# A complex linear recurrence on one Trainium2 core: four of ten elementwise instructions of each group on GpSimd, with a second buffer for two tiles

## What is computed

```
x: 8 sequences of 256 tokens, 128 channels
lambda = exp(-nu + i theta),  gamma = sqrt(1 - |lambda|^2 + eps)
Bu[t]  = gamma * (B_re + i B_im) x[t]
h[t]   = lambda * h[t-1] + Bu[t]                    (complex, per channel)
out[t] = Re(C h[t]) + D_skip * x[t]
x      = layernorm(x + out)
```

## Time and profile before

| | |
|---|---|
| median of three runs | 1337.15 us |
| lowest, highest | 1335.71, 1341.49 us |
| span of the profiled execution (first to last instruction) | 1318.2 us |
| TensorE busy, share of the span | 1096.4 us, 83% |
| VectorE busy | 801.6 us, 61% |
| ScalarE busy | 534.2 us, 41% |
| GpSimd busy | 379.6 us, 29% |

### The profile page before, as it was taken

One profiled execution on the slowest core, in us unless ns is written; L12 is line 12 of the kernel. 1 busy time (PEld: TensorE's weight loads), 2 busy tenths in 40 slices (PEclk: granted clock), 3 DMA queues, 4 the chain that ended last, 5 costly groups with the idle time before them and its releaser, 6 DMA issues. The chain is left out here.

```text
span 1318.2 us, 28739 instructions
## 1 busy us (share of the span) xinstructions
PE 1096.4 (83%) x9627; PEld 802.6 (61%) x9627; DVE 801.6 (61%) x2791; ACT 534.2 (41%) x1167; POOL 379.6 (29%) x515
## 2 busy tenths in 40 slices
PE   8999987784998884799977757887887989999891
PEld 4656555674466851556634324553766979899791
DVE  6566355344588868745577774456962757767323
ACT  4366642474543322222222123222123756658481
POOL 2344416443100720000000115540023434534351
PEclk9899998998998576899987968998877999999996
DMA  1210359222000059078644265553902212031212
GB/s 50 48 39 3 130 173 369 62 64 76 1 2 2 5 190 333 10 162 206 250 160 146 58 203 120 130 117 103 347 14 68 69 35 65 22 78 39 65 45 64
DMA packets 112895, 135.88 MB, mean 103 GB/s; under 512 B 16899, under 2 KB 78422, under 8 KB 112096
## 3 DMA queue, kind: packets, MB, share of 16 engines
q1 hardware_dynamic: 100160, 119.26, 29.3%
q0 software_dynamic: 12592, 14.79, 4.5%
HBM read 67.92 MB, written 69.32 MB: 104 GB/s over the span
## 5 line engine op out<-in xcount | busy, mean ns | idle before, releaser
L2125 PE MATMUL m_psY<-large,m_hT 128*128 (+2 forms) x992 | 139.3, 284 | 0.0
L2125 PEld LDWEIGHTS m_psY<-large,m_hT 128*128 128x128 f32 x992 | 126.9, 191 | 0.1
L2045 POOL DMA_INDIRECT rows<-m_ys,m_slot x93 | 90.8, 976 | 114.9 <-DVE m_slot L2280 104.7
L572 DVE TENSOR_REDUCE at_peaks<-at_ps 128x3 f32<-128x384 f32 x128 | 65.4, 551 | 49.3 <-PE at_ps L335 49.3
L484 ACT ACTIVATE at_PT<-at_ps,at_bias 128x384 f32<-128x384 f32 x128 | 67.4, 578 | 51.7 <-PE at_ps L345 51.6
L2181 ACT ACTIVATE m_hT<-m_psH 128x512 f32<-128x512 f32 x124 | 73.7, 594 | 32.1 <-PE m_psH L2107 31.8
L131 PE MATMUL ln_idle<-blank,ident 128*128 128x512 f32 x112 | 55.3, 651 | 27.5 <-PEq L890 14.8
L279 POOL TENSOR_SCALAR_AFFINE_SELECT at_PT<-at_PT 128x256 f32<-128x256 f32 x128 | 55.1, 432 | 75.3 <-ACT at_PT L484 71.5
L1444 POOL IOTA row_no<- 128x1 f32 x1 | 0.1, 132 | 256.0 <-SPq L687 256.0
L2107 PE MATMUL m_psH<-m_xT,large 128*128 128x128 f32 x512 | 69.2, 280 | 0.0
L2107 PEld LDWEIGHTS m_psH<-m_xT,large 128*128 128x128 f32 x512 | 65.0, 198 | 0.0
(11 more groups left out here) (709 smaller groups left out, 2764.9 us busy)
## 6 DMA issues: line engine op xcount, KB each, us to landing
rows<-blank SPq DMA_DIRECT2D x16, 2448.0 KB, 21.9
m_xs<-rows SPq DMA_DIRECT2D x124, 76.5 KB, 2.0
pair_rows<-blank SPq DMA_DIRECT2D x1, 8320.0 KB, 25.8
large<-in_L_attn_firs SPq DMA_DIRECT2D x4, 2048.0 KB, 20.4
large<-comb_rows SPq DMA_DIRECT2D x64, 128.0 KB, 5.5
se_wu<-in_L_ffn_up SPq DMA_DIRECT2D x32, 192.0 KB, 2.6
W2T<-in_L_ffn_down_turned SPq DMA_DIRECT2D x1, 4096.0 KB, 12.4
large<-in_L_ffn_up SPq DMA_DIRECT2D x4, 1024.0 KB, 8.2
```

Source lines behind the costliest of these rows:

```text
L572: nc.vector.tensor_reduce(peaks[:, b % 2, n, :], psS[:, u % TILES, 0:CAUSAL].rearrange("p (x c) -> p x c", c=P), AX.X, ALU.max).then_inc(r ...
L2045: pool.indirect_dma_start(k.rows[(layer + 1) % 2], bass.IndirectOffsetOnAxis(slot[:, q:q + 1], 0), ys[:, q, :], None, bounds_check=E3 * N ...
L2125: m = nc.tensor.matmul(psY[b][:, 0:wide], hT[b][:, c * P:(c + 1) * P], w, start=(c == 0), stop=(c == C - 1))
```

## The change

The four products that use the imaginary half of the turned input and one of the four products of the turning back go to GpSimd: `m[:, 2]` and `m[:, 3]`, their difference `gi`, and part 2 (`sr` times sin). VectorE keeps six elementwise instructions and the two scans. `gi` and `sr` have two buffers instead of one. GpSimd does the three instructions of group g+1 ahead of part 2 of group g. VectorE makes part 0 right after the scan of `sr`, then waits for `gi`, scans `si` and makes parts 1 and 3. TensorE takes the parts in the order 0, 2, 1, 3. ScalarE waits for GpSimd's `gi` too before it overwrites `br` and `bi`. There are new counts between the engines: `turned_im` (gi done), `scanned` (sr done), `parted_im` (part 2 done), and `made`, by which GpSimd waits for its own products.

```diff
-        gr, gi, sr, si = (sb(n, [P, 2, SEQ]) for n in ("gr", "gi", "sr", "si"))
+        gr, si = (sb(n, [P, 2, SEQ]) for n in ("gr", "si"))
+        gi, sr = (sb(n, [P, 2, 2, SEQ]) for n in ("gi", "sr"))
...
-                for i, c in enumerate(("Cr", "Cn", "Ci", "Ci")):
-                    pe.wait_ge(*parted.at(4 * g + i + 1))
+                for i, c, done in ((0, "Cr", parted.at(3 * g + 1)), (2, "Ci", parted_im.at(g + 1)),
+                                   (1, "Cn", parted.at(3 * g + 2)), (3, "Ci", parted.at(3 * g + 3))):
+                    pe.wait_ge(*done)
...
                 if g >= 2:
                     act.wait_ge(*turned_back.at(g - 1))
+                    act.wait_ge(*turned_im.at(g - 1))
...
+        @block.gpsimd
+        def _(pool):
+            def turn_im(g):
+                b = g % 2
+                pool.wait_ge(*scaled.at(g + 1))
+                if g:
+                    pool.wait_ge(*turned_im.at(g))
+                nc.gpsimd.tensor_tensor(m[:, 2], bi[:, b], C, ALU.mult).then_inc(made.sem, 1)
+                nc.gpsimd.tensor_tensor(m[:, 3], br[:, b], S, ALU.mult).then_inc(made.sem, 1)
+                pool.wait_ge(*made.at(2 * g + 2))
+                if g >= 2:
+                    pool.wait_ge(*parted.at(3 * (g - 2) + 3))
+                nc.gpsimd.tensor_tensor(gi[:, b], m[:, 2], m[:, 3], ALU.subtract).then_inc(turned_im.sem, 1)
+
+            turn_im(0)
+            for g in range(PAIRS):
+                if g + 1 < PAIRS:
+                    turn_im(g + 1)
+                pool.wait_ge(*scanned.at(g + 1))
+                if g >= 2:
+                    pool.wait_ge(*out_done.at(g - 1))
+                nc.gpsimd.tensor_tensor(parts[:, g % 2, 2], sr[:, g % 2], S, ALU.mult).then_inc(parted_im.sem, 1)
...
-                nc.vector.tensor_tensor(m[:, 1], bi[:, b], S, ALU.mult)
-                nc.vector.tensor_tensor(m[:, 2], bi[:, b], C, ALU.mult)
-                nc.vector.tensor_tensor(m[:, 3], br[:, b], S, ALU.mult).then_inc(turned_back.sem, 1)
+                nc.vector.tensor_tensor(m[:, 1], bi[:, b], S, ALU.mult).then_inc(turned_back.sem, 1)
                 dve.drain()
                 nc.vector.tensor_tensor(gr[:], m[:, 0], m[:, 1], ALU.add)
-                nc.vector.tensor_tensor(gi[:], m[:, 2], m[:, 3], ALU.subtract)
-                dve.drain()
-                nc.vector.tensor_tensor_scan(flat(sr[:]), flat(w["decay"][:]), flat(gr[:]), 0.0, ALU.mult, ALU.add)
-                nc.vector.tensor_tensor_scan(flat(si[:]), flat(w["decay"][:]), flat(gi[:]), 0.0, ALU.mult, ALU.add)
+                dve.drain()
+                if g >= 2:
+                    dve.wait_ge(*parted_im.at(g - 1))
+                nc.vector.tensor_tensor_scan(flat(sr[:, b]), flat(w["decay"][:]), flat(gr[:]), 0.0, ALU.mult, ALU.add)\
+                    .then_inc(scanned.sem, 1)
                 dve.drain()
                 if g >= 2:
                     dve.wait_ge(*out_done.at(g - 1))
-                for i, (state, turn) in enumerate(((sr, C), (si, S), (sr, S), (si, C))):
-                    nc.vector.tensor_tensor(parts[:, b, i], state[:], turn, ALU.mult).then_inc(parted.sem, 1)
+                nc.vector.tensor_tensor(parts[:, b, 0], sr[:, b], C, ALU.mult).then_inc(parted.sem, 1)
+                dve.wait_ge(*turned_im.at(g + 1))
+                nc.vector.tensor_tensor_scan(flat(si[:]), flat(w["decay"][:]), flat(gi[:, b]), 0.0, ALU.mult, ALU.add)
+                dve.drain()
+                nc.vector.tensor_tensor(parts[:, b, 1], si[:], S, ALU.mult).then_inc(parted.sem, 1)
+                nc.vector.tensor_tensor(parts[:, b, 3], si[:], C, ALU.mult).then_inc(parted.sem, 1)
```

More of the change, by code:

```diff
@@ L3318, in lru_stage @@
     projected, scaled, out_done = k.tally("pr_projected"), k.tally("ln_scaled"), k.tally("lr_out_done")
+    made = k.tally("made")
     turned_back, parted = k.tally("lr_turned_back"), k.tally("lr_parted")
+    turned_im, scanned, parted_im = k.tally("turned"), k.tally("copied"), k.tally("parts_done")
     fold_in, folded, folded_out = k.tally("l3_fold_in"), k.tally("l3_folded"), k.tally("l3_folded_out")
@@ L3397, in _ @@
                 nc.scalar.activation(k.X[:, 4 * g:4 * g + 4, :].rearrange("p t d -> p (t d)"), psO[:, g, :], ACT.Copy)
+        C, S = each(w["cos"]), each(w["sin"])
+        @block.gpsimd
[19 more added lines that the diff above has]
+                nc.gpsimd.tensor_tensor(parts[:, g % 2, 2], sr[:, g % 2], S, ALU.mult).then_inc(parted_im.sem, 1)
         @block.vector
         def _(dve):
-            C, S = each(w["cos"]), each(w["sin"])
             for g in range(PAIRS):
@@ L3423, in lru_stage @@
     scaled.close(PAIRS)
+    made.close(2 * PAIRS)
+    for t in (turned_im, scanned, parted_im):
+        t.close(PAIRS)
     fold_in.close(32)
```

## The result

| | before | changed |
|---|---|---|
| median | 1337.3 us (20 runs) | 1346.14 us (20 runs) |
| lowest, highest | 1330.54, 1347.18 | 1339.6, 1353.31 |
| ratio, 95% interval | | 1.0065 (1.0047 to 1.0082) |

The change makes the kernel slower by 8.8 us; the interval is 6.3 to 11.0 us. The forecast was +6.8, 1344.0 us, in a range of 1340.5 to 1348.5. One of the twelve executions of c_after took 3605.6 us, for a reason that no run shows; it is in no ratio, and the median of the other eleven is 1342.15 us.

What follows compares the result with a forecast made beforehand. VectorE was taken to bound the stage; its chain grows from 35.2 to 42.8 us (25.5 + 18.7 - 1.4), +7.6, and TensorE's tail gives -0.8: 1337.15 + 6.8 = 1344.0 us, range 1340.5 to 1348.5.

Steps and rivals of the forecast that it cites:

- Which engine bounds the stage, and that the engines exclude each other: VectorE bounds the stage at 8.78 us a group, and only one of VectorE and GpSimd works at any time; 72%.
- That scans block too: VectorE's scans also hold GpSimd up; the rival that they don't gave -0.9 us, 1336.2 us, 8%.
- The predicted signs: In the changed profile: many VectorE instructions near 1.8 us, GpSimd's over 1.26, stage end near 966, tail within 1.5 us.
- 1345.3: End of the sum, in us, if each of GpSimd's sixteen instructions cost its full 1.26 us by the Trainium skill's rule.
- VectorE's remaining work, 25.5 us: VectorE's chain in the stage after four elementwise instructions of each group leave: 4 x (8.78 - 2.40) = 25.5 us.
- GpSimd's part, 18.7 less 1.4 for what hides, so 17.3: Added to VectorE's chain: sixteen GpSimd instructions at 1.17 us, 18.7, less 1.4 for VectorE's start-up and three hidden drains.
- The 1.17 less 0.06 of VectorE's start-up: Each GpSimd instruction excludes VectorE for 1.17 us, between 1.12 and 1.23; each engine change hides 0.06 of VectorE's start-up.
- TensorE's tail, -0.8: TensorE's work behind VectorE's last part falls from 2.1 to about 1.3 us, since only parts 1 and 3 come close together.
- The mechanism: Rival: TensorE idles, drops to its lower clock in groups 0 to 2, and VectorE waits for `out_done`: 1348 us, 12%.
- The 19 us around the span: Time outside the profile's span of 1318.2 us, taken as untouched, so the change adds directly to the median of 1337.15.
- The rival of no blocking, 1329.6 us: VectorE's chain is 25.5 us alone and the stage ends about 951.9, held by SyncE's loads: -7.5 us, 8%.
- The chances: Against differences within 0.5% (6.7 us), the whole kernel's time was given faster 0.08, same 0.38, slower 0.54.

Runs made afterwards that it cites:

- c_after: The changed kernel run once more beside the control: chain 42.44 us, stage 46.38 us, median 1342.38 us, ratio 1.0048.
- e1b_writes: Changed kernel with GpSimd's sixteen products replaced by memsets, same order and waits, gi and part 2 not computed: chain 26.98 us, tail 9.28 us, ratio 0.9947.
- e3_psum: Changed kernel with VectorE's first two products of a group reading psR and psI in PSUM, times gamma: chain 39.44 us, ratio 1.0027.
- e7_one: Against e2_order, GpSimd makes part 2 alone, right after the scan of sr: chain 38.04 us, ratio 1.0022.
- e6_under: e5_psum_all with GpSimd making parts 2 and 3 of groups 0 to 2 under VectorE's next products from PSUM: chain 33.24 us, ratio 0.9924, again 0.9954.
- e2_order: Changed kernel without its GpSimd block: VectorE makes all ten products and both scans in the changed order: chain 35.96 us, ratio 1.0003.
- e4b_fill3: Changed kernel with three unused matmuls on TensorE ahead of the last group's parts: chain 42.40 us, tail 1.52 us, ratio 1.0012.
- c_before: The kernel before run once more as a control: chain 35.22 us, tail 3.71 us, median 1334.94 us, ratio 0.9987.
- e5_psum_all: GpSimd idle, VectorE makes all four first products from PSUM without ScalarE's copies, parts in order 0, 2, 1, 3: chain 36.83 us, ratio 0.9996.

## Why the prediction was right, point by point

**Which engine bounds the stage, and that the engines exclude each other.** Right, and the step that carried the forecast. The eight instructions of L2788 in another stage told it before the change was built; e1b_writes, e3_psum, e7_one and e6_under confirm it from four sides: no hold where GpSimd only writes, none where VectorE reads PSUM, one for each product moved, and a gain where the two kinds are kept apart. That scans block too, read from one short instruction, is seen in the changed kernel: GpSimd's product that met the scan of `sr` took 1.99 us. The predicted signs came too, but for the tail within 1.5 us, which was 3.02.

The rule of the Trainium skill ("SBUF — State Buffer", "Who interferes with whom") holds in kind, with GpSimd's writes free and VectorE's PSUM reads free. Of its "whole instruction" a little hides: VectorE's recorded wait behind a GpSimd product of 1.26 us is 1.11 us in e7_one. (With 1.26 for each the prediction's own terms give 1345.4 us, not its 1345.3.)

**VectorE's remaining work, 25.5 us.** 0.8 too low. "The number of drains stays at three" was wrong, there are four, and e2_order shows their price as 0.76. Without the wait for TensorE, e1b_writes has 26.98 - 0.71 = 26.27.

**GpSimd's part, 18.7 less 1.4 for what hides, so 17.3.** Measured: 42.43 - 26.27 = 16.2 us, 1.01 for each of sixteen. The 1.17 less 0.06 of VectorE's start-up was right: 1.11 in e7_one, and 1.07 to 1.11 in ten of the sixteen in the changed kernel. What was mis-sized is the drains that fall under a GpSimd instruction: it took three. The other six VectorE instructions that were held up all came behind a drain (in group 0 `gr`, the scan of `sr` and parts 0 and 1, in group 1 `gr` and part 1), and their waits are 0.82 to 0.90 us. (Part 0 of the later groups waited 1.11 behind a drain too, but there GpSimd's product began only with it.) That the drain ran while GpSimd worked is argued from this and not tested by a run of its own. The two errors offset each other, 0.8 too low above and 1.1 too high here, and that is luck: chain 42.8 forecast, 42.43 measured.

**TensorE's tail, -0.8.** This step had the wrong sign against the profile that it was forecast from: +0.9 (3.02 against 2.09). Against the second profile of before (3.71) it is -0.7, by luck, since there the kernel before has the slow tail. The step took eight products at the full clock. After an idle time of 2.83 us they weren't, and e4b_fill3 gives what the step would have been with the clock kept up: 1.52, or -0.6. (Four sets of products take 3.84 us by the earlier trace rows, which the prediction rounds to 3.9.) The mechanism stood among the rivals, but for groups 0 to 2, where it did no harm (`out_done` was never late); it came in the last group. That is the difference between +6.8 and the +8.4 of the first pair of profiles: chain -0.4, tail +1.7, and 0.3 for a later start of VectorE. Times of the whole kernel, +8.8 and +6.4 with intervals of 5 us and more, can't tell the two apart.

**The 19 us around the span.** They are not start and end work. The changed kernel's profile, with a span of 1347.9 us, is of an execution of 1349.6 us, so 1.7 us lie outside it, and in c_before it is 1329.06 against 1327.3. The profile of before, with its 1318.2 us, must be of an execution of about 1320 us, shorter than any of the twenty. The sum does not suffer, since it adds a difference to the median.

**The rival of no blocking, 1329.6 us.** Its price was wrong as well. SyncE's loads were named as the floor, but e1b_writes shows TensorE as the next bound, with a stage only 1.0 us shorter than before. By that run, a GpSimd that excluded nobody would hardly have gained anything in this order (an estimate: GpSimd's writes end part 2 of group 0 at 943.10, 9.0 us behind VectorE's start, and seven products of 1.26 take 8.8): part 2 comes behind the next group's input, and TensorE waits for it.

**The chances.** Slower by over 0.5% is what was measured (0.65%; 0.48% in the repeat). The case lay close to that line, as was said.

## What to carry to other kernels

Before elementwise work is moved from VectorE to GpSimd, look at where the operands are and not at how idle GpSimd is: with two SBUF inputs on one side and SBUF reads on the other, a product of 128x512 moved saved 0.60 us and cost 1.0 to 1.1. It pays where VectorE meanwhile has an input in PSUM, and then it pays in full. Look in the trace for an instruction whose longest is several times its shortest, with no releaser named, and see what another engine did at that moment; and price a shorter chain against the next engine in line before counting the gain.

## What was not expected of the hardware

The two engines shared strictly by turns where both always had something to do: in group 0 of the changed kernel seven of eight VectorE instructions wait for exactly one of GpSimd's, all seven of GpSimd's last 1.59 to 2.06 us in place of 1.26, and neither engine is ever held up for two.

TensorE did not always slow down at once after an idle time. In e2_order, behind 2.75 us of idling, the first eight products still took 1.17 us, the next two sets 1.89 and 1.90, and the last 1.08. The granted clock was 1.00 in the idle time, 0.97 in the first set, 0.50 in the next two and 0.98 in the last:

```profile
959.21 1.17 PE L3377 MATMUL lr_psO<-lr_Cr,lr_parts 128*128 128x128 f32 x8 [2.75 <-DVE lr_parts L3422]
960.21 1.89 PE L3377 MATMUL lr_psO<-lr_Ci,lr_parts 128*128 128x128 f32 x8
961.89 1.90 PE L3377 MATMUL lr_psO<-lr_Cn,lr_parts 128*128 128x128 f32 x8
963.60 1.08 PE L3377 MATMUL lr_psO<-lr_Ci,lr_parts 128*128 128x128 f32 x8
```

In e5_psum_all it was the same behind 2.87 us: 1.16, then 1.59, 2.08 and 1.25. Behind longer idle times the first eight were slow already: 2.08 us behind 4.13 and behind the 3.73 of e1b_writes. Idle times of 1.01 us (the first profile of the kernel before) and 1.71 us (e3_psum, ahead of its last parts) were followed by products at 1.06 to 1.16 us throughout. The kernel before showed both, a fast end and a slow one, in two executions.
